# Two expert layers on one core: the order of a step, the size of the table loads, dropped waits and smaller last groups

## The reference, cut to what matters

```python
# first expert layer: top 2 of 14, plus two shared experts
h = xn * jax.lax.rsqrt(ms + RMS_EPS) * rw
return jax.nn.silu(h @ W1) @ W2
...
routed_out = jnp.einsum('end,ne->nd', routed, masked)
return (routed_out + shared).reshape(B, T, D)
# second expert layer: top 2 of 8
hmid = jax.nn.gelu(jnp.einsum('th,ehf->tef', hn2, w1), approximate=False)
y = jnp.einsum('tef,efh->th', hmid * gates[:, :, None], w2)
return x1 + y.reshape(s, b, h)
# then, over all
x = _layernorm(x + ..., axis=-1)
```

## Time and profile before

| what | value |
|---|---|
| median of 3 runs | 2053.09 us (2051.61 to 2054.27) |
| profiled execution | 2048.72 us, its span 2047.0 us |
| busy in the span | PE 1745.5 us (85%), PEld 1410.6 (69%), DVE 1415.0 (69%), ACT 1336.0 (65%), POOL 1052.7 (51%) |
| `route` | first gather 921.4, last output copied 1144.8 us |
| `route_pairs` | first gather 1831.2, last scatter issued 2036.9 us |
| granted TensorE clock | mean 0.95 |

### The profile page before, as it was taken

How to read it: one execution, slowest core, us unless ns; L and a number is a source line. 1 busy time by engine, 2 the same in 40 slices (tenths; PEclk the granted TensorE clock), 3 DMA queues, 4 the chain that set the end, 5 groups by cost and what they waited for, 6 DMA issues and landing times. The chain is left out here.

```text
span 2047.0 us, 51429 instructions
## 1 busy us (share of the span) xinstructions
PE 1745.5 (85%) x15897; PEld 1410.6 (69%) x15928; DVE 1415.0 (69%) x5778; ACT 1336.0 (65%) x3320; POOL 1052.7 (51%) x1384
## 2 busy tenths in 40 slices
PE   7799999999999998899999478888769999459884
PEld 6555555555555556788999467777648998438784
DVE  1377878887878785583422279999659888565775
ACT  3488888888888873424455358888658898326553
POOL 2133333333333323117667578887539899717544
PEclk9899999999999998999999789999979999759998
DMA  7899999999999964006576312222221221278542
GB/s 220 281 291 317 315 313 307 314 308 321 306 318 313 309 241 144 22 1 177 169 198 197 96 30 60 60 60 56 47 71 41 54 53 41 44 131 227 173 143 73
DMA packets 222087, 350.07 MB, mean 171 GB/s; under 512 B 56928, under 2 KB 169568, under 8 KB 221312
## 3 DMA queue, kind: packets, MB, share of 16 engines
q1 hardware_dynamic: 187024, 305.34, 47.6%
q0 software_dynamic: 14144, 31.16, 6.3%
q10 hardware_dynamic: 20656, 10.29, 1.7%
HBM read 160.82 MB, written 144.67 MB: 149 GB/s over the span
## 5 line engine op out<-in xcount | busy, mean ns | idle before, releaser
L183 POOL TENSOR_SCALAR_AFFINE_SELECT heads_raw_relative<-heads_raw_relative 128x508 f32<-128x508 f32 x256 | 166.7, 675 | 497.3 <-ACT heads_raw_relative L568 457.4
L568 ACT COPY heads_raw_relative<-heads_rel_bank 128x768 f32<-128x768 f32 x247 | 198.6, 804 | 122.5 <-PE heads_rel_bank L463 122.3
L492 PE MATMUL attend_turn_bank<-ident,attend_score 128*128 128x128 f32 x1536 | 231.3, 286 | 20.9 <-ACT attend_prob_t L574 19.6
L492 PEld LDWEIGHTS attend_turn_bank<-ident,attend_score 128*128 128x128 f32 x1536 | 163.5, 142 | 117.3 <-ACT attend_prob_t L574 68.5
L574 ACT ACTIVATE attend_prob_t<-attend_turn_bank 128x384 f32<-128x384 f32 x512 | 224.8, 500 | 6.6 <-PE attend_turn_bank L492 6.6
L578 ACT ACTIVATE attend_score<-attend_score,attend_extreme 128x128 f32<-128x128 f32 x512 | 215.7, 421 | 9.1 <-DVE attend_extreme L625 8.8
L625 DVE CUSTOM_DVE_ANT_0 attend_score<-attend_score_bank,heads_relative 128x256 f32<-128x256 f32 x512 | 214.8, 420 | 0.0
L622 DVE CUSTOM_DVE_ANT_0 attend_score<-attend_score_bank,heads_relative 128x128 f32<-128x128 f32 x512 | 146.7, 286 | 74.6 <-PE attend_score_bank L463 49.9
L631 DVE TENSOR_SCALAR attend_score<-attend_score,attend_extreme 128x256 f32<-128x256 f32 x512 | 195.5, 382 | 0.0
L1423 POOL DMA_INDIRECT moe_route_rows_sb<-tokens,moe_taken x154 | 145.8, 947 | 70.2 <-PE moe_route_bank L1445 40.6
L463 PE MATMUL attend_score_bank<-heads_qk 32*128 32x256 f32 x1024 | 155.3, 379 | 0.0
(11 more groups left out here) (438 smaller groups left out, 5154.9 us busy)
## 6 DMA issues: line engine op xcount, KB each, us to landing
shear<-heads_raw_relative SPq DMA_DIRECT2D x128, 768.0 KB, 5.9
heads_relative<-shear SPq DMA_DIRECT2D x128, 768.0 KB, 5.6
duo_w_now<-moe_w SPq DMA_DIRECT2D x158, 129.0 KB
moe_route_w_now<-moe_w SPq DMA_DIRECT2D x154, 129.0 KB
expert_out<-moe_route_y ACTq DMA_DIRECT2D x38, 256.0 KB
qk_heads<-heads_qk_out SPq DMA_DIRECT2D x32, 256.0 KB, 4.0
heads_qk<-qk_heads SPq DMA_DIRECT2D x128, 64.0 KB
pair_rows<-groups SPq DMA_DIRECT2D x16, 260.0 KB, 9.1
```

The lines of the kernel that those rows point to most:

```text
L183: m = nc.gpsimd.affine_select(out=future, in_=future, compare_op=ALU.is_ge, fill=-BIG, base=1 - P, pattern=[[0, QUAD], [1, P - 1]], channe ...
L492: mm = nc.tensor.transpose(bank[:, j * P:(j + 1) * P], score[:, (h - LAG) % RING, j * P:(j + 1) * P], c.ident[:, :])
L568: nc.scalar.copy(raw[:, ring, 2 * half:2 * half + 2, :], r_bank[:, :, 0:W]).then_inc(rel_moved, 1)
```

## The change

In the first expert layer the order of two pieces of work in a step is exchanged, on TensorE (hidden before turn) and on ScalarE (activate before rows_transposed), and three waits are left out, each contained in one that the engine has already passed in the new order. In the second layer the same is done, the table loads fill four registers in place of eight (and so are twice as many), the tiles' loads now fall two units apart from the experts', and the experts' load stands directly ahead of the output. The last 16 tiles are normalized in groups of four, four, four, two, two where they were eight, four, two, two; up to tile 48 the groups of eight stay. `KEEP_AFTER` goes from 5 to 4.

```diff
@@ route, TensorE
             def turn(s):
                 pe.wait_ge(taken[s % TAKEN], 16 * (s // TAKEN + 1))
-                wait_past(pe, rows_ready, s - TURNS + 1)
+                if 0 < s < 3:
+                    pe.wait_ge(rows_ready, s)
...
+                if s + 2 < STEPS:
+                    hidden(s + 2)
                 if s + 3 < STEPS:
                     turn(s + 3)
-                if s + 2 < STEPS:
-                    hidden(s + 2)
                 output(s, experts[s % LOADED])
@@ route, ScalarE
             def rows_transposed(s):
                 act.wait_ge(turned, s + 1)
-                if s >= DEEP:
-                    act.wait_ge(hid_made, s - DEEP + 1)
...
                 act.wait_ge(hid_made, s + 1)
-                if s >= DEEP:
-                    act.wait_ge(y_made, s - DEEP + 1)
...
             for s in range(STEPS):
+                if s + 2 < STEPS:
+                    activate(s + 2)
                 if s + 3 < STEPS:
                     rows_transposed(s + 3)
-                if s + 2 < STEPS:
-                    activate(s + 2)
@@ route_pairs
-    S, RING, DEEP, AHEAD, LOAD = UNITS, 12, 4, 2, UNITS_LOADED
-    PORTION, KEEP_AFTER = 8, 5
-    ends = list(range(8, NT - 8 + 1, 8)) + [NT - 4, NT - 2, NT]
+    S, RING, DEEP, AHEAD = UNITS, 12, 4, 2
+    PORTION, KEEP_AFTER = 8, 4
+    ends = list(range(8, NT - 16 + 1, 8)) + [NT - 12, NT - 8, NT - 4, NT - 2, NT]
...
-                pairs.experts[0:1, u:u + LOAD], [engine], min_val=0, max_val=ex.n - 1,
+                pairs.experts[0:1, u:u + LOADED], [engine], min_val=0, max_val=ex.n - 1,
@@ route_pairs, TensorE
             def turn(t):
                 gathered(pe, t)
-                wait_past(pe, rows_ready, t - 1)
+                if t == 2:
+                    pe.wait_ge(rows_ready, 1)
...
             def hidden(u, tile):
-                pe.wait_ge(rows_ready, needed(u) + 1)
-                wait_past(pe, hid_ready, u - 2)
+                if u == 0 or needed(u) > needed(u - 1):
+                    pe.wait_ge(rows_ready, needed(u) + 1)
...
             for u in range(S):
-                if u % LOAD == 0:
-                    experts = experts_of(mybir.EngineType.PE, u)
+                if u + AHEAD < S:
+                    if (u + AHEAD) % LOADED == 0:
+                        tiles = tiles_of(mybir.EngineType.PE, u + AHEAD)
+                    hidden(u + AHEAD, tiles[(u + AHEAD) % LOADED])
                 if u % 2 == 0 and u // 2 + 3 < NT:
                     turn(u // 2 + 3)
-                if u + AHEAD < S:
-                    if (u + AHEAD) % LOAD == 0:
-                        tiles = tiles_of(mybir.EngineType.PE, u + AHEAD)
-                    hidden(u + AHEAD, tiles[(u + AHEAD) % LOAD])
-                output(u, experts[u % LOAD])
+                if u % LOADED == 0:
+                    experts = experts_of(mybir.EngineType.PE, u)
+                output(u, experts[u % LOADED])
@@ route_pairs, ScalarE
                 act.wait_ge(hid_made, u + 1)
-                wait_past(act, y_made, u - DEEP + 1)
...
             for u in range(S - AHEAD):
+                activate(u + AHEAD)
                 if u % 2 == 0 and u // 2 + 3 < NT:
                     rows_transposed(u // 2 + 3)
-                activate(u + AHEAD)
```

15 lines of the change are left out of this document (7 added, 8 removed).

## The result

The changed kernel takes 2080.1 us in the median of four runs (2073.9 to 2083.2), the kernel before 2052.8 on the same chip (2051.6 to 2054.3). The ratio is 1.0121, with a 95% interval of 1.0100 to 1.0141: slower by 21 to 29 us (the two medians alone stand 27.3 us apart). The forecast was 2082. The profiled execution has a span of 2077.8 us against 2047.0.

What follows compares the result with a forecast made beforehand. TensorE's summed matrix work bounds the first layer; in the second, TensorE gains count only where VectorE isn't last. Terms 34 - 2 - 3 = +29 us on 2053.1 gave 2082 us, range 2063 to 2103.

Steps and rivals of the forecast that it cites:

- The loop in the first layer: First layer: hidden matmuls, activation, copy, next hidden matmuls form a once-per-step loop of 1.39 us; +34 us.
- ScalarE's delay behind the shared hidden work: First layer: the routed activation waits for the shared activation, about 0.2 us more once in twelve steps.
- The idle 0.2 to 0.4 us ahead of the hidden matmuls: First layer, sign in the profile: TensorE idles this long between steps, put down to ScalarE's copy.
- The rival that the loop doesn't bind: First layer: real latencies are shorter, down to 1.0 us a step, so stalls vanish; 2040 us, chance 0.09.
- The clock: Rival, first layer: TensorE's granted clock falls, the loop becomes 2.1 us, +90 on top; 2172 us, chance 0.04.
- The waits: First layer: leaving out one wait a step on TensorE and two on ScalarE changes nothing.
- The second layer's order: Second layer: hidden ahead of transpose and activate ahead of copy close no loop; nothing gained or lost.
- Loads of four: Second layer: smaller loads, fewer waits and the root step one unit earlier together give -2 us, ends -10 and +12.
- the rival of +0.3 for each added load (+12): Second layer: each of 40 added loads shows by 0.3 us, +12 instead of -2; 2096 us, chance 0.05.
- The smaller last groups: End of second layer: POOL's queue empties before the last pair, last scatter one scatter (1.28 us) after it; -3 us.
- the added chain of eleven root steps: Second layer, VectorE: 2.2 us, far enough ahead of the end to be made up; if not, +1.
- The -5 for the second layer: Second layer: sum of -2 for loads, fewer waits and earlier root step, and -3 for the last groups.

Runs made afterwards that it cites:

- order_only: Kernel before with only the second layer's changed order on TensorE and ScalarE, loads of eight and all waits kept: 2049.9 us, ratio 0.9993.
- groups_only: Kernel before with only the smaller last groups and the rows taken up one unit earlier: 2053.4 us, ratio 1.0019.
- swap_tensor: Kernel before with the first layer's swap on TensorE alone, ScalarE still copying first, all waits kept: 2061.3 us, ratio 1.0052.
- swap_waits_kept: Kernel before with the first layer's swap on both engines, all waits kept: one run, 2222.4 us, beside 2208.0 for the kernel before.
- swap_scalar: Kernel before with the first layer's swap on ScalarE alone, TensorE's old order and all waits kept: 2101.8 us, ratio 1.0241.

## Why the prediction came out

**The loop in the first layer** was the forecast's main term, and right in kind and nearly in size. Forecast and measured: to the activation 0.75 and 0.75, to the copy 0.28 and 0.28, the copy 0.27 and 0.26, the handover 0.09 and 0.07; the step 1.39 and 1.36. Twelve unlisted steps 19.6 and 19.16, listed 19.95 and 19.60. Over the layer this makes +28.5 in place of +34: the term was 5.5 us too large. Ten times 0.03 is 0.3 of each difference. The rest of the unlisted one is next to the shared work: the step with the shared output matmuls took 2.78 us where 2.87 was reckoned, and ScalarE's delay behind the shared hidden work was 0.15, not 0.2. The idle 0.2 to 0.4 us ahead of the hidden matmuls are there (0.28), put down to "issue" rather than to the copy as I had said.

**The rival that the loop doesn't bind** needed 1.0 us or less; it was 1.36. **The clock** stayed at 1.00 in the first layer with TensorE 94% busy (108.97 of 116). **The waits** left out: the loop is the same 1.36 with them and without.

**The second layer's order** was put at nothing. No loop closed, which was the point, but order_only shows -1.7 us. A small miss, on the good side, and its cause is not known.

**Loads of four** were put at -2, with -10 and +12 as ends. Alone they measured -2.1 behind unit 8, and about -1 in the first eight units (9.8 to 10.9 against 10.6 to 12.2). That a load costs by its values holds (0.33 at the least for four, 0.59 for eight), and the rival of +0.3 for each added load (+12) is out.

**The smaller last groups** are where two steps failed. The prediction had the last scatter one scatter (1.28 us) behind the pair, less than 2 us behind the last row, for -3. It came 2.2 us behind the last row, and -2.1 was gained. The step left out the way from VectorE to POOL: in all fourteen profiles no scatter starts sooner than 0.79 us behind the end of its row, and most of those that POOL waits for start just then. The last pair in the changed kernel shows it. The first of the two rows ends at 2065.45, POOL has been free since 2065.76, and the scatter starts at 2066.24:

```profile
2066.24 0.98 POOL L1891 DMA_INDIRECT out<-duo_rows_sb,pair_take  x1 [0.48 <-DVE duo_rows_sb L2052]
```

So 0.35 for the row, 0.79 and 1.28 lie between the start of the pair and the last scatter. The other step was that the added chain of eleven root steps, 2.2 us, lies far enough ahead of the end to be made up. It isn't: the eight units in which it stands took 2.4 us more. With three output banks TensorE stands still too while VectorE works on the chain (1.18 us in groups_only), and none of it was made up in the units behind. The term was -3 and measured +0.3 in the tail, +1.6 for the whole edit.

**The total.** +28.5 - 4.1 = +24.4 us in the profiles, and 1.0121 times 2052.8 is +24.8. The forecast had +29, the upper edge of what the interval allows (21 to 29). That it came within 2 us of the median (2082 for 2080.1) owes something to chance: the first layer was 5.5 us too dear, while the medians lie 27.3 us apart, and in the profiled execution an untouched stretch was 5.3 us longer through the clock. The -5 for the second layer is luck in its parts: the order gave 1.7 us that weren't forecast, and the last groups, forecast at -3, gave nothing. The direction and the mechanism of the main term are not luck; the experiments on the loop bear them out.

## What to carry to other kernels

Where two engines hand work to each other once per step, write down for each hand-over how many steps lie between making and using, and follow the queue order round: the swap put the copy behind the activation and made a wait that had 0.31 us of slack into a loop of 1.36 us, and the same edit with the copy one step further ahead cost 7.8 us in the layer in place of 28.5. The length of such a loop could be summed beforehand from starts in a timeline, here to within 0.03 us for the change and 0.06 for the swap on ScalarE alone. Before calling a step "made up later", look how many banks the other engine can fill meanwhile, and whether there is slack behind it; and when an engine gets faster, look who is next, here POOL's scatters at 1.29 us each.

## What the runs showed of the hardware

- The granted clock of TensorE in one and the same stretch of an unchanged stage was 1.00 in one execution and 0.50 in another, and that stretch took from 47.6 to 52.9 us over fourteen profiles, and no link to what was changed shows. One profile against another can't be trusted below some 5 us in the total. Stage lengths agreed better: unit 8 to the last scatter within 0.6 us over four profiles with the old second layer, and within 1.0 over three with the changed one.
- A wait that is released by ScalarE's copy gave TensorE's next weight load 0.07 us behind the copy's end where it was the hidden matmuls' and another wait stood behind it (changed kernel, swap_tensor, swap_waits_kept), and 0.11 where it was the transpose's last wait (swap_scalar).
- An instruction on ScalarE starts before the one ahead has ended: the copy 0.28 us behind the start of an activation of 256 columns that lasts 0.38.
- POOL started no scatter sooner than 0.79 us behind the end of the row that VectorE made, in all fourteen profiles, and most of those that it waited for just then; scatters back to back start every 1.29 us, of which POOL is busy 0.98.
